# A six-layer windowed-attention stack: values of a head pair in zero-filled blocks, one 128-row product for both heads in the mix

## The reference, cut to what matters

```python
for i in range(DEPTH):                       # 6 layers
    x = attn_layer(shift_tokens(x), Wqkv[i], q_scale[i], k_scale[i], Wo[i]) + x
    x = ffn_layer(shift_tokens(x), ln_g[i], ln_b[i], W1[i], b1[i], W2[i], b2[i]) + x

def local_attention(q, k, v):                # windows of 32 tokens
    bk2, bv2 = (look(bk), look(bv))          # keys, values of the window before and of this one: 64
    sim = jnp.einsum('bhwie,bhwje->bhwij', bq, bk2) * QK_SCALE
    sim = jnp.where(mask, -jnp.finfo(sim.dtype).max, sim)
    attn = jax.nn.softmax(sim, -1)
    return jnp.einsum('bhwij,bhwje->bhwie', attn, bv2)
```

## Time and profile before

| | |
|---|---|
| median of 3 runs | 2190.03 us (2189.59 to 2193.81) |
| the profiled execution | 2187.69 us, its span 2185.9 us |
| TensorE, matmuls | 1743.0 us busy (80%), 20107 |
| TensorE, weight loads | 1085.1 us (50%), 20107 |
| VectorE | 1350.5 us (62%) |
| ScalarE | 894.3 us (41%) |
| GpSimd | 635.3 us (29%) |
| mean granted TensorE clock | 0.891 |

### The profile page before, as it was taken

How to read it: one execution, slowest core, us unless ns; L and a number is a source line. 1 busy time by engine, 2 the same in 40 slices (tenths; PEclk the granted TensorE clock), 3 DMA queues, 4 the chain that set the end, 5 groups by cost and what they waited for, 6 DMA issues and landing times. The chain is left out here.

```text
span 2185.9 us, 47509 instructions
## 1 busy us (share of the span) xinstructions
PE 1743.0 (80%) x20107; PEld 1085.1 (50%) x20107; DVE 1350.5 (62%) x2406; ACT 894.3 (41%) x1609; POOL 635.3 (29%) x994
## 2 busy tenths in 40 slices
PE   2005167699776889898898888999887999999999
PEld 1002045443443556555565556555554677676433
DVE  5796746421275878788778777788663556554311
ACT  1001023233223555556456455556553454553332
POOL 0000012000023756666557556656630000000000
PEclk6556579699798999999999999999896999999799
DMA  1000000001004343333334333333311000000100
GB/s 31 21 0 11 1 26 10 15 29 29 27 0 120 108 115 89 102 102 94 103 96 107 89 96 99 98 88 86 89 29 39 1 1 1 1 1 1 30 29 29
DMA packets 66259, 111.70 MB, mean 51 GB/s; under 512 B 9936, under 2 KB 29238, under 8 KB 66050
## 3 DMA queue, kind: packets, MB, share of 16 engines
q1 hardware_dynamic: 65234, 108.44, 18.3%
q10 hardware_dynamic: 816, 0.24, 0.0%
HBM read 82.14 MB, written 26.03 MB: 49 GB/s over the span
## 5 line engine op out<-in xcount | busy, mean ns | idle before, releaser
L1319 POOL TENSOR_TENSOR st_r<-st_r,st_t 128x512 f32<-128x512 f32 x192 | 243.3, 1270 | 295.2 <-DVE st_t L1286 295.0
L1243 PE MATMUL PS<-st_wqkv,st_xs 128*128 128x512 f32 x576 | 311.1, 625 | 16.6 <-DVE st_xs L1496 9.1
L1334 POOL TENSOR_TENSOR st_r<-st_r,st_gy 128x512 f32<-128x512 f32 x192 | 198.7, 1065 | 3.8
L1278 DVE TENSOR_TENSOR st_r<-PS,st_rot 128x512 f32<-128x512 f32 x192 | 129.8, 676 | 107.9 <-ACT st_sqh L1262 107.3
L2035 ACT ACTIVATE la_p<-PS,la_nmx 128x589 f32<-128x589 f32 x128 | 95.0, 747 | 133.5 <-DVE la_nmx L2066 133.5
L2066 DVE TENSOR_REDUCE la_nmx<-PS 128x1 f32<-128x589 f32 x128 | 92.7, 766 | 91.8 <-PE PS L1928 91.8
L1262 ACT ACTIVATE st_sqh<-PS 128x512 f32<-128x512 f32 x192 | 114.3, 595 | 73.5 <-PE PS L1243 73.3
L1063 DVE TENSOR_TENSOR m_y<-PS,m_wb 128x512 f32<-128x512 f32 x32 | 22.1, 691 | 187.7 <-ACT m_wb L1036 187.7
L641 POOL MEMSET l_s<- 128x144 f32 x2 | 0.5, 225 | 459.8 <-DVE x L531 270.0
L1346 PE MATMUL PS<-cst,st_r 128*128 128x128 f32 x768 | 119.2, 290 | 16.0 <-issue 11.6
L1286 DVE TENSOR_TENSOR st_t<-PS,st_rot 128x512 f32<-128x512 f32 x192 | 130.4, 679 | 0.0
(11 more groups left out here) (315 smaller groups left out, 3677.0 us busy)
## 6 DMA issues: line engine op xcount, KB each, us to landing
st_vv<-st_v_out SPq DMA_DIRECT2D x168, 256.0 KB, 4.8
st_v_out<-st_v SPq DMA_DIRECT2D x48, 512.0 KB, 2.6
st_wqkv<-in_st_wqkv SPq DMA_DIRECT2D x18, 512.0 KB, 7.5
m_w<-in_m_w SPq DMA_DIRECT2D x32, 256.0 KB, 3.0
st_vv<-st_v_out SPq DMA_DIRECT2D x24, 192.0 KB, 3.3
st_wo<-in_st_wo SPq DMA_DIRECT2D x6, 512.0 KB
st_w<-in_st_w SPq DMA_DIRECT2D x6, 341.0 KB
la_wc<-in_la_wc SPq DMA_DIRECT2D x1, 1344.0 KB, 6.4
```

Of the source, the lines that this page charges most:

```text
L1243: pe.matmul(PS[:, 2 + m % 2, :], self.xs[:, b, P * t:P * t + P], self.wqkv[:, l % 2, k, 512 * half:512 * half + 512], start=True, stop=Tru ...
L1278: dve.tensor_tensor(h3(self.r[:, t % 2, c, :]), h3(ps), self.rot[:, k, 0, t, :].unsqueeze(1) .broadcast_to([P, 8, D2]), ALU.mult)
L1319: pool.tensor_tensor(r, r, self.t2[:, c % 2, :], ALU.add).then_inc(self.added, 1)
L1334: pool.tensor_tensor(r, r, y[:, 8 * c:8 * c + 8].unsqueeze(2).broadcast_to([P, 8, D2]), ALU.mult)\
```

## The change

st_vv no longer has a place for every window. It has two slots of four windows, used by even and odd T. In each, the values of a pair of heads lie in two blocks of columns: block e holds values in rows 64e to 64e + 63 alone, and zeros in the others. So one product of the 128 rows of weights (both heads) by 128 columns gives both heads' results side by side. The mix has 32 products instead of 64, each with 128 rows, 32 columns of weights and 128 moving columns, in tiles (0, 32w); heads of pairs 0 to 3 go to bank 0, 4 to 7 to bank 1. VectorE's sum and output follow the new order of heads. SyncE's loads of tile T wait for the mix of T-2 (pv_done at least T-1) and are six, since the last window of the tile before is loaded again: two of 64 KB, two of 256, two of 192; at t = 0 they are four. The zeros are set once, by GpSimd, over all of st_vv.

```diff
--- before.py
+++ after.py
@@ -1111,7 +1111,7 @@
             self.v = s("v", [P, 2, INNER])
             self.v_out = dram("st_v_out", (4, P, INNER))
 
-            self.vv = s("vv", [P, S // WIN, INNER // 2])
+            self.vv = s("vv", [P, 8, 2, INNER // 2])
             self.e = s("e", [P, 8, 2, 2 * WIN])
             self.pT = s("pT", [P, 8, P])
             self.mx = s("mx", [P, 16])
@@ -1176,24 +1176,32 @@
         W = 3 * 16
         WF = 5 * 16
 
+        def v_load(self, sp, T, e, h, first, count, to, signal):
+
+            rows = slice(64 * e + WIN * h, 64 * e + WIN * h + WIN)
+            src = view(self.v_out, ((T % 4) * P + WIN * first) * INNER + 512 * e,
+                       [[INNER, WIN], [WIN * INNER, count], [1, 512]])
+            sp.dma_start(self.vv[rows, to:to + count, e, :], src).then_inc(self.vshift[signal], 16)
+
         def sp_shift(self, sp, T):
 
-            u, t = divmod(T, self.TILES)
+            t = T % self.TILES
+            at = 4 * (T % 2)
 
             sp.wait_ge(self.v_evac, T * 2 + 2)
-            if u > 0:
+            if T >= 4:
                 sp.wait_ge(self.pv_done, T - 3)
             sp.dma_start(self.v_out[t], self.v[:, t % 2, :]).then_inc(self.v_stored, 16)
-            if u > 0 and t < 3:
-
-                sp.wait_ge(self.pv_done, T - 2)
+
+            if T >= 2:
+                sp.wait_ge(self.pv_done, T - 1)
+            if t > 0:
+                for e in range(2):
+                    self.v_load(sp, T - 1, e, 0, 3, 1, at, t)
             sp.wait_ge(self.v_stored, T * 16 + 16)
             for e in range(2):
-                for h in range(2):
-                    first, count = 4 * t + 1 - h, 4 - (t == 3 and h == 0)
-                    rows = slice(64 * e + WIN * h, 64 * e + WIN * h + WIN)
-                    src = view(self.v_out, t * P * INNER + 512 * e, [[INNER, WIN], [WIN * INNER, count], [1, 512]])
-                    sp.dma_start(self.vv[rows, first:first + count, :], src).then_inc(self.vshift[t], 16)
+                self.v_load(sp, T, e, 1, 0, 4, at, t)
+                self.v_load(sp, T, e, 0, 0, 3, at + 1, t)
 
         def sp(self, sp):
             sp.dma_start(self.base[:, :, :, :, :], io["st_base"]).then_inc(self.c_in, 16)
@@ -1396,8 +1404,7 @@
 
         def dve_sum(self, dve, T):
             dve.wait_ge(self.exps, T + 1)
-            dve.tensor_reduce(self.den[:, :].rearrange("p (e c) -> p e c", e=2),
-                              self.e[:, :, :, :].rearrange("p c e k -> p e c k"), X, ALU.add)\
+            dve.tensor_reduce(self.den[:, :], self.e[:, :, :, :].rearrange("p c e k -> p (c e) k"), X, ALU.add)\
                .then_inc(self.den_ready, 1)
             dve.wait_ge(self.den_ready, T + 1)
             dve.reciprocal(self.rden[:, T % 2, :], self.den[:, :]).then_inc(self.rden_ready, 1)
@@ -1426,15 +1433,13 @@
 
             u, t = divmod(T, self.TILES)
             pe.wait_ge(self.p_evac, 2 * T + 2)
-            pe.wait_ge(self.vshift[t], (u + 1) * 64)
+            pe.wait_ge(self.vshift[t], (u + 1) * (64 if t == 0 else 96))
             for c in range(8):
                 for w in range(4):
-                    for e in range(2):
-                        rows = slice(64 * e, 64 * e + 64)
-                        g = slice(WIN * w, WIN * w + WIN)
-                        mm = pe.matmul(PS[g, e, D2 * c:D2 * c + D2], self.pT[rows, c, g],
-                                       self.vv[rows, 4 * t + w, D2 * c:D2 * c + D2], start=True, stop=True,
-                                       tile_position=(64 * e, WIN * w), skip_group_check=True)
+                    g = slice(WIN * w, WIN * w + WIN)
+                    mm = pe.matmul(PS[g, c // 4, P * (c % 4):P * (c % 4) + P], self.pT[:, c, g],
+                                   self.vv[:, 4 * (T % 2) + w, :, D2 * c:D2 * c + D2], start=True, stop=True,
+                                   tile_position=(0, WIN * w), skip_group_check=True)
             mm.then_inc(self.pv_done, 1)
 
         def dve_out(self, dve, T):
@@ -1442,9 +1447,9 @@
             dve.wait_ge(self.rden_ready, T + 1)
             if T > 0:
                 dve.wait_ge(self.o_turned, 2 * T)
-            dve.tensor_tensor(self.on[:, :, :, :].rearrange("p c e d -> p e c d"),
-                              PS[:, 0:2, :].rearrange("p e (c d) -> p e c d", c=8),
-                              self.rden[:, T % 2, :].rearrange("p (e c) -> p e c", e=2).unsqueeze(3)
+            dve.tensor_tensor(self.on[:, :, :, :].rearrange("p (b c) e d -> p b (c e) d", b=2),
+                              PS[:, 0:2, :].rearrange("p b (h d) -> p b h d", h=8),
+                              self.rden[:, T % 2, :].rearrange("p (b h) -> p b h", b=2).unsqueeze(3)
                               .broadcast_to([P, 2, 8, D2]), ALU.mult).then_inc(self.on_ready, 1)
 
         def pe_turn_o(self, pe, T, half):
@@ -1742,7 +1747,7 @@
         def pool(self, pool):
 
             for k, what in enumerate((self.xs[64:P, :, 0:1], self.xf[64:P, 0:1], self.kT[:, :, 0:WIN],
-                                      self.vv[0:WIN, 0, :], self.vv[64:64 + WIN, 0, :])):
+                                      self.vv[:, 0:4, :, :], self.vv[:, 4:8, :, :])):
                 pool.memset(what, 0.0).then_inc(self.set_up, 1)
                 pool.wait_ge(self.set_up, k + 1)
             for T in range(self.N):
```

## The result

The changed kernel takes 2169.53 us (median of 5 runs, 2168.74 to 2173.06) against 2189.59 us (5 runs, 2183.94 to 2193.81): a ratio of 0.9931, 95% interval 0.9906 to 0.9957 (the two medians alone lie 20.1 us, 0.9%, apart). It is 0.7% faster, where 2198 us was forecast; it lies inside the range on record (2160 to 2226) but outside the forecast's own (2188 to 2212). The profiled execution has a span of 2171.1 us. The stack began 5.9 us later in this execution; that part of the code is unchanged, and over the 19 profiles of this study the beginning lies between 676.1 and 684.7 us without regard to the kernel.

What follows compares the result with a forecast made beforehand. The prediction took the stack to be bound by TensorE, with VectorE close behind. Longer mix +13 and holes -4 gave +9 us on the 2190.03 us median, about 2199 (2198 put down), range 2160 to 2226.

Steps and rivals of the forecast that it cites:

- The mix: TensorE's mix products: 1.80 us a tile, limited by streaming, 0.39 us more than before, 18.7 us in 48 tiles.
- The share that reaches the end: Part of the longer mix that shows in the total time: 0.7, so +13 us, bounds +9 to +19.
- The holes: TensorE's idle time waiting for instruction pages (256 instructions each): 53 us against 57, so -4 us.
- the 8 late mix ends 12 in sum: Eight instruction-page ends late in a mix, their next pages delayed by the load burst: 12 us of holes together.
- 7 of the ends in the short stretch in full (28): Page ends between mix and next scores: seven with holes of 3.4 to 3.9 us, 28 us; four others 2 us.
- the early ends behind the scores 9, and 2 for a doubled end: Page ends soon after the scores: 9 us of holes; a doubled end in the second tile: 2 us.
- The price of a hole: Time in the total for each us of TensorE's holes: counted one for one, with no term for the clock.
- The clearing: GpSimd's larger memsets of st_vv at the stack's start: hidden behind VectorE's work, 0 us, at worst +2.
- VectorE's views: The changed views in VectorE's sum and output: below 0.05 us a tile either way, 0 +/- 2 us.
- The sum: All terms together: +13 for the longer mix, -4 for the holes, +9 us, about 2199 us.
- Rival (b): Thinner TensorE stream leaves pages in time despite the moved burst: holes 57 to 16 us, about 2162 us; chance 0.28.
- Rival (e): Instruction pages cost nothing of their own, so only the longer mix shows: +13, 2203 us; chance 0.12.

Runs made afterwards that it cites:

- e3: The changed kernel with 128 already fulfilled waits added among the products of each mix, four to a product; 2388.5 us, ratio 1.093.
- e2: The changed kernel with the st_vv loads early again, through a third set of blocks and a single buffer for v; 2138.6 us, ratio 0.979.
- e8: e2 with each mix product of 128 columns split into two of 64, over the same rows and zeros; 2177.4 us, ratio 0.997.
- e7: The kernel before with st_vv loads of 64 of 512 columns from the fifth tile on, the mix partly using old values; 2140.5 us, ratio 0.980.
- e15: e6 with 56 tiny products (112 instructions) ahead of the stack, to shift the page ends; 2136.7 us, ratio 0.978.
- e12: e6 with the four large st_vv loads of a tile issued one by one, each after the last landed; 2143.8 us, ratio 0.979.
- e16: e6 with 96 tiny products (192 instructions) ahead of the stack, to shift the page ends; 2141.2 us, ratio 0.979.
- e6: e2 with only the blocks that must stay zero cleared, by GpSimd and ScalarE at the same time; 2138.4 us, ratio 0.980.

## Why the prediction was wrong, step by step

**The mix: right in kind, a little short.** 64 records, limited by streaming, all four column tiles overlapping: 1.89 us, not 1.80 (+0.48 us a tile, 23 us in all, not 18.7). The row of L1956 was the right one. **The share that reaches the end** held: a fit through the 18 profiles of the table without e3, stack less start (first clearing to first projection) = 899.4 + 1.29 x holes + 0.78 x 48 x (mix run - 1.48), leaves 2.9 us of scatter (standard errors 0.05 and 0.04 of the two factors). 0.78 for a forecast of 0.7; the term is +18, not +13. The bounds, +9 to +19, held it.

**The holes: this is the step that failed.** 53 was forecast, 33.5 came. Term by term, with the page ends where they had been counted to fall:
- "the 8 late mix ends 12 in sum": they cost 0.45 us. I let every request start 1 us after its page end and so into the burst. At the tile of 1018.92 the page ends in the mix at 1020.48, 0.4 us before the end of its run; q8's packet lies in the window 1020.6 to 1020.9, with q1 silent, since the loads cannot be issued before the mix is done:

```profile
1018.92 1.96 PE L1440 MATMUL PS<-st_vv,st_pT 128*32 128x128 f32 x64
...
1024.53 1.49 PE L1380 MATMUL PS<-st_kT,st_qT 64*32 64x64 f32 x128
```

```profile
q8 instruction: 1, 0.02, 26.4%
```

The scores of 1024.53, with the next page end in them, run through without a hole. Of the eight packets seven start 0.3 to 0.9 us after their page end. Two ends lie within the last six instructions of a mix: the packet of the one at 1003.5 is held for 4.8 us and leaves a hole of 0.45 us, that of the one at 1209.4 is not. The moved wait that I had booked as a cost shields these ends.
- "7 of the ends in the short stretch in full (28)" and 2 for the others: they cost about 23, and the mechanism is as described. The tile of 763.78, page end at 766.66, in the windows 766.8 to 771.9 and 771.9 to 772.3:

```profile
q1 hardware_dynamic: 579, 1.29, 102.1%
```

```profile
q8 instruction: 1, 0.02, 16.7%
```

```profile
768.59 1.42 PE L1380 MATMUL PS<-st_kT,st_qT 64*32 64x64 f32 x120
774.60 0.44 PE L1380 MATMUL PS<-st_kT,st_qT 64*32 64x64 f32 x8 [4.58 <-issue]
```

The packet starts 5.4 us after the page end and is usable 2.6 us later (ahead of it on q1 are here, too, 512 KB of the next layer's weights). The holes of these ends are 0.3 to 4.6 us long, not always 3.4 to 3.9: where the end stands late in the burst, less of it is ahead, and where the next 256 instructions take longer, they cover more of the delay (after the end at 986.99 the packet starts 3.9 us late, the instructions take 6.0 us, and the hole is 0.31).
- "the early ends behind the scores 9, and 2 for a doubled end": about 10. Right.

**The price of a hole was left at 1.** The fit gives 1.29 us of stack for a us of hole. Part of that may be the clock: between 720 and 1585 us the granted clock is at the 1.2 GHz level for 56 us before, 27 after and 3 in e2. I had seen the lower clock of tiles with holes and put no term on it. By the fit the 23.5 us of holes that went are worth 30 us, where the forecast had 4 us for 4. How much of the 0.29 is the clock, and how much the queue behind a hole, the runs don't separate.

**The clearing** was booked at nothing since it ends before the first instruction that waits for it. That looked at the wrong instruction: the copies that run ahead of it, without any wait, were locked out. 1.4 us, within the 2 that I had as the worst. **VectorE's views** cost nothing: 1225, 1220, 1217 and 1210 ns against 1224, 1219, 1218 and 1209.

**The sum** with these sizes: +18 - 30 + 1 = -11 us; the stack measured -18.3 and the median -20.1. The fit's scatter covers the stack's 7 us (before lies 4 above it, the changed kernel 3 below), but what they are made of stays open. The sum on record was +9 (2199 us; 2198 was put down). Of the 29 us between it and the median the holes and their price account for 26, the longer mix and the clearing work against that with 6, and some 9 stay unexplained. Rival (b), the thin stream leaves the pages in time, at 2162, was the nearer one in time, though its 16 us of holes were too few by nearly as much as my 53 were too many, and it named the mechanism; what I held against it was one late packet of the kernel before, in a mix of twice as many instructions. Rival (e), pages cost nothing, falls: e8 against e2 has 39 us on the count of instructions, and e7 has 44 us (ratio 0.980) on the bytes ahead of the packets. By the Trainium skill ("Runtime: NRT & Kernel Launch", instruction fetch mechanics) such a crossing is mostly hidden. By count most are hidden here too, but not by cost: before, 38 of the stack's some 124 crossings show, with 57.0 us in sum.

## What to carry to other kernels

Count the instructions of a busy TensorE stream as bytes that must arrive, and look at which transfers stand ahead of them: here that was worth up to some 50 us of 2190, and two lines that issue the loads one by one got 38 of it without touching the arithmetic. When a change moves a burst, ask not only what it now collides with but which page requests it can no longer overtake; a burst released by the end of a run leaves the requests inside the run free. And judge a kernel with such holes at more than one place of its page ends before calling a difference under 1% its own.

## What the hardware did that was not expected

- A fulfilled wait in a run of small products costs 45 ns, four times a record of the old mix (11 ns).
- VectorE's copies between SBUF tensors stop while GpSimd clears, 0.43 us becoming up to 3.69; its operations that read PSUM do not.
- Half the instructions in the mix, with the loads as early as before, were worth 2.1% (e2), though each mix got longer by a third.
- The best versions that compute the whole stack, e15, e2, e12, e16 and e6 (ratios 0.978 to 0.980, not told apart), are 2.0 to 2.2% faster than before and 1.3 to 1.5% faster than the change.
